# Last batch: routing steps, ranks and row sends reordered against halves of the shared expert

## The reference, cut to what matters

```python
x = x + xattn(layernorm(x), ctx, ctx, ...)
f = layernorm(x)
logits = f @ Wg
gates = softmax over the two largest logits, 0 elsewhere
y = sum over e of (silu(f @ W1[e] + b1[e]) * (f @ W11[e] + b11[e]) @ W2[e] + b2[e]) * gates[:, e]
z = silu(f @ Ws1 + bs1) * (f @ Ws11 + bs11) @ Ws2 + bs2
x = x + y + z
```

## Time and profile before

| what | value |
|---|---|
| median of 3 runs | 305.14 us (305.01 to 306.45) |
| the profiled execution | 304.97 us, its span 303.2 us |
| PE busy | 272.4 us (90% of the span) |
| DVE busy | 206.7 us (68%) |
| ACT busy | 150.2 us (50%) |
| POOL busy | 141.9 us (47%) |

### The profile page before, as it was taken

How to read it: one execution, slowest core, us unless ns; L and a number is a source line. 1 busy time by engine, 2 the same in 40 slices (tenths; PEclk the granted TensorE clock), 3 DMA queues, 4 the chain that set the end, 5 groups by cost and what they waited for, 6 DMA issues and landing times.

```text
span 303.2 us, 6139 instructions
## 1 busy us (share of the span) xinstructions
PE 272.4 (90%) x1829; PEld 204.7 (68%) x1845; DVE 206.7 (68%) x724; ACT 150.2 (50%) x316; POOL 141.9 (47%) x228
## 2 busy tenths in 40 slices
PE   7777899999998999989998999999789999999910
PEld 7554555666565665565564467898689999999900
DVE  3869455665857678775796468773267787878863
ACT  3434787655664574746554754322145454544500
POOL 3484614654233307843347303755026566666740
PEclk9999999999999999999999999999999999999975
DMA  6999940929890000100001100118625959777446
GB/s 207 378 366 395 406 190 1 108 33 136 308 383 11 2 1 0 38 18 20 0 2 36 36 1 8 51 42 269 196 55 151 288 186 286 254 237 229 105 191 208
DMA packets 28495, 44.22 MB, mean 146 GB/s; under 512 B 2752, under 2 KB 16192, under 8 KB 28464
## 3 DMA queue, kind: packets, MB, share of 16 engines
q1 hardware_dynamic: 21808, 36.52, 36.0%
q0 software_dynamic: 6656, 7.31, 10.9%
HBM read 27.00 MB, written 14.73 MB: 138 GB/s over the span
## 4 chain that ended last, share of the span: by engine, by line
PE 64%; DVE 14%; DMA 8%; POOL 5%; issue 5%; ACT 3%; POOLq 0%; DVEq 0%; ACTq 0%; SPq 0%
PE ps L1470 6%; PE ps L1476 6%; PE ps L1487 6%; DVE mpad L587 6%; PE ps L1190 5%; PE ps L1218 5%; PE ps L1232 5%; PE ps L1191 4%; PE ps L1228 4%; POOL slot_rows L866 3%; PE ps L1216 3%; PE ps L1203 3%; DMA result_rows<-yo,dest 3%; PE ps L1139 2%; PE ps L1141 2%
## 5 line engine op out<-in xcount | busy, mean ns | idle before, releaser
L587 DVE TENSOR_REDUCE mpad<-ps 128x2 f32<-128x312 f32 x128 | 55.8, 477 | 35.5 <-PE ps L1191 35.2
L937 POOL DMA_INDIRECT result_rows<-yo,dest x47 | 45.3, 964 | 39.0 <-DVE yo L790 38.1
L816 POOL TENSOR_SCALAR ks<-k_stack,cst 128x160 fp32r<-128x160 f32 x64 | 30.0, 483 | 70.9 <-DVE k_stack L560 70.9
L1002 ACT ACTIVATE pf<-ps 128x512 f32<-128x512 f32 x80 | 46.6, 597 | 15.0 <-PE ps L1232 10.8
L1191 PE MATMUL ps<-ks,qs 96*128 96x312 f32 x128 | 47.2, 411 | 0.0
L1190 PE MATMUL ps<-mq_b,identb 128*128 128x312 bf16 x128 | 38.1, 303 | 5.6 <-POOL ks L816 3.2
L866 POOL DMA_INDIRECT slot_rows<-xr,slot x32 | 31.5, 984 | 14.2 <-issue 13.9
L1218 PE MATMUL ps<-qs,ks 128*128 128x512 f32 x64 | 37.1, 582 | 0.0
L1190 PEld LDWEIGHTS ps<-mq_b,identb 128*128 128x128 bf16 x128 | 12.3, 96 | 34.9 <-issue 30.5
L1126 ACT ACTIVATE e_s<-ps,wu 128x128 f32<-128x128 f32 x62 | 19.4, 364 | 21.8 <-PE ps L1470 21.8
L1487 PE MATMUL ps<-wd,e_h 128*128 (+1 forms) x188 | 28.7, 276 | 0.6 <-DVE yo L790 0.6
(11 more groups left out here) (194 smaller groups left out, 602.6 us busy)
## 6 DMA issues: line engine op xcount, KB each, us to landing
wu<-w_biased SPq DMA_DIRECT2D x31, 322.0 KB, 3.9
wr<-w_up SPq DMA_DIRECT2D x1, 5152.0 KB, 24.7
w_biased<-wr SPq DMA_DIRECT2D x1, 5152.0 KB, 16.9
slot_rows<-zero SPq DMA_DIRECT2D x1, 3120.0 KB, 26.9
xg<-slot_rows SPq DMA_DIRECT2D x12, 260.0 KB, 3.9
wd<-w_down SPq DMA_DIRECT2D x1, 2048.0 KB, 12.0
xo<-result_rows SPq DMA_DIRECT2D x3, 512.0 KB, 5.3
xs<-bor POOLq DMA_DIRECT2D x1, 1024.0 KB, 11.3
```

The lines of the kernel that those rows point to most:

```text
L587: dve.tensor_reduce(mpad[:, m % 2, q, 96 + 2 * a:98 + 2 * a], ps[:, KS_ + a, 0:2 * SKM].rearrange("p (c k) -> p c k", c=2), AX.X, ALU.max, ...
L816: pool.tensor_scalar(ks[:, HG * (m % 4) + j, :], k_stack[:, m % 2, :], cst[:, C_SELM + j:C_SELM + j + 1], cst[:, C_SELO + j:C_SELO + j + 1 ...
L937: pool.indirect_dma_start(out=result_dram[:, :], out_offset=bass.IndirectOffsetOnAxis(ap=dest[:, n:n + 1], axis=0), in_=yo[:, n % 4, :], i ...
L1002: act.activation(pf[:, n % RP, :], ps[:, ST_ + n % 2, :], ACT.Exp, scale=DK ** -0.5).then_inc(exp_done, 1)
```

## The change

Nothing is computed differently, and no instruction is added. Orders change on four engines: on DVE the slots of batch 2 go ahead, the statistics and the normalization of batch 3 go ahead of products, and the slots of batch 3 are put around product 6, ahead of product 7; on POOL three sends of batch 2 go ahead of the inverse deviation; on ACT one small activation is moved; on PE the turn, the logits and the ranks go ahead of halves, the second layer of batch 2 is split by three halves, and the wait for the last add moves behind the third up-projection.

```diff
--- before.py
+++ after.py
@@ -721,31 +721,32 @@
 
             last = B - 1
             gates(last - 1)
-            slots(last - 1, 0)
+            for step in range(3):
+                slots(last - 1, step)
             normalize(last, NG - 1)
-            slots(last - 1, 1)
+            slots(last - 1, 3)
             linear_half(0)
-            slots(last - 1, 2)
-            slots(last - 1, 3)
+            slots(last - 1, 4)
             add_attention(last, 0)
+            batch_statistics(last, 0)
             linear_half(1)
-            batch_statistics(last, 0)
             linear_half(2)
+            next_blocks(last - 1)
+            batch_norm(last, 0)
             linear_half(3)
-            batch_norm(last, 0)
-            slots(last - 1, 4)
+            batch_low(last, 0)
             linear_half(4)
-            batch_low(last, 0)
-            next_blocks(last - 1)
-            linear_half(5)
             read_logits(last)
             for step in range(4):
                 pick(last, step)
+            linear_half(5)
+            gates(last)
+            for step in range(3):
+                slots(last, step)
             linear_half(6)
-            gates(last)
+            for step in range(3, 5):
+                slots(last, step)
             linear_half(7)
-            for step in range(5):
-                slots(last, step)
             linear_half(8)
             tile_experts()
             linear_half(9)
@@ -927,8 +928,9 @@
             split_weights(1)
             for b in range(B):
                 batch(b)
+            send(B - 2, range(3))
             batch_inverse_std(B - 1, 0)
-            send(B - 2, range(2 * QT))
+            send(B - 2, range(3, 2 * QT))
             send(B - 1, range(2 * QT))
 
 
@@ -1103,8 +1105,8 @@
             batch_high(B - 1, 0)
             silu(5)
             copy_rows(B - 1, 0)
+            gate_exp(B - 1)
             silu(6)
-            gate_exp(B - 1)
             silu(7)
             for k in range(8, 16):
                 silu(k)
@@ -1418,14 +1420,14 @@
             first(2)
             first(3)
             first(4)
+            turn_normed(B - 1, 0)
             first(5)
-            turn_normed(B - 1, 0)
+            logits(B - 1, 0)
             second(0, (0, 1))
-            logits(B - 1, 0)
+            first(6)
+            rank_rows(B - 1)
             second(0, (2, 3))
-            first(6)
             first(7)
-            rank_rows(B - 1)
             first(8)
             first(9)
             second(1, (0, 1))
@@ -1435,9 +1437,9 @@
             first(11)
             first(12)
             second(2, (0, 1))
-            second(2, (2, 3))
             for k in range(13, 16):
                 first(k)
+            second(2, (2, 3))
             second(3, (0, 1))
 
 
@@ -1492,7 +1494,6 @@
             pe.wait_ge(x2_done, B - 1)
             turn_rows(0)
             second(3, (2, 3))
-            pe.wait_ge(x2_done, B)
             pe.wait_ge(tile_known, 1)
             pe.wait_ge(ld_d, 32)
             experts = {0: expert_of(0)}
@@ -1503,6 +1504,8 @@
                     up(n)
                 if 1 <= n < RUN:
                     experts[n] = expert_of(n)
+                if n == 2:
+                    pe.wait_ge(x2_done, B)
                 if n >= 2:
                     down(n - 2, experts.pop(n - 2))
 
```

## The result

The changed kernel takes **308.01 us** (median of 17 runs, 306.36 to 310.47) against 305.37 us for the kernel before in its 17 runs: a ratio of 1.0091, 95% interval 1.0066 to 1.0117. It is slower by more than the half per cent that can be told. The forecast was 306.7 with a range up to 307.9: the direction of the sum was right, the size was missed just beyond the edge.

The account below looks back on a forecast made before the run. Bound: the chain of sends, row load, turn and experts. A later tile list delays the row load; with the moved wait, experts at 222.1 instead of 220.57, +1.55; 304.75 becomes 306.5, median 0.17 above: 306.7, range 305.3 to 307.9.

Parts of the forecast that it names:

- The order of the passage: Attention to experts: times of the reordered steps, from batch 2's slots at 180.3 to the tile list published at 206.5.
- other signs of being right: Rows issued right behind the eighth weight load, near 216, long after the last send; no wait between last piece and experts.
- The rows' landing: First row load behind the weight loads: lands 3.9 us after its issue at 215.9, so the turn is at 219.9.
- The last piece: Second-layer piece on PE between the turn and the experts: 1.75 us, within the 2.2 from turn to experts.
- What moves 220.57 moves the end by as much: Start of the experts, 220.57 before: PE's expert matmuls follow without a gap, so a shift there moves the end equally.
- Stops added up: PE ahead of the tile list: new stops 1.3 + 0.8 + 0.3 + 1.1, less 0.2, put the one-row matmul 3.25 us later.
- The gain of these sends is nil: POOL's three early sends of batch 2: without them all of batch 2's sends would be over before 195 anyway.
- The moved wait: Wait for the last add, behind the third up-projection: turn to experts 2.2 instead of 3.20 us, one microsecond won.
- Floor landing: Rival: the row load lands 2.9 us after issue, 305.7 us in all; chance 0.20.
- the list in time: Rival "faster": PE's stops don't reach the tile list, published by 203.3; sends decide again, 303.2 us; chance 0.07.
- The port rule: Rival "slower still": DVE's normalization and POOL's send shut each other out, row load to tile list 0.97 later, 307.7; chance 0.15.
- that rival's condition: Sign for the slower rival, 307.7 us: it decides as soon as a send starts ahead of the normalization; chance 0.15.

Follow-up runs that it names:

- the second profile: The changed kernel, nothing altered, timed and profiled once more: 307.53 us against 305.19 for the kernel before, ratio 1.0095; the profiled execution took 306.27 us.
- the first profile: The changed kernel's profile from its first timing: execution of 307.83 us, span 306.0 us, against 304.97 and 303.2 us for the kernel before.

## Why the prediction missed

**The order of the passage: right.** The forecast is named first, the measured time behind it. Slots of batch 2 at 180.3 (180.05), inverse deviation behind three sends done at 186.0 (185.7), half 3 at 183.5 (183.12), turn at 187.2 (187.07), logits at 189.4 (189.22), ranks at 193.6 (193.34), slots at 198.7 (198.44), half 9 at 199.5 (199.24), one-row matmul at 205.95 (205.70), list at 206.5 (206.05 and 0.20). With the earlier start of 0.39 added back, each is within 0.3 us. The stops ahead of halves 3 and 9 were 1.42 and 0.84 us for 1.3 and 1.1. Its other signs of being right came true too: the row load behind the eighth weight load, the sends long landed, no wait between the last piece and the experts.

**The rows' landing: mis-sized, and this is the step that failed first.** The prediction took 3.9 us, the middle of twelve issues, on the ground that three sends fewer run beside it. Measured: 4.87, and 4.61 in the second profile. The twelve issues were the wrong sample, as they reach down to 272 us, far into the experts, and most don't stand behind eight weight loads: in the changed kernel the engines are 0.92 busy over 216 to 218.4 and 0.71 in the 2 us after, and with that the rows land. An earlier issue did not help either (5.90 with the sends put back, though the engines were 0.41 busy over 218 to 220 us there, for 0.87 in the changed kernel), so the backlog alone does not give the number. The bound of 5.7 in the prediction held all but that one; the value inside it was chosen too low.

**The last piece: priced at the wrong clock.** "Experts at 219.9 + 2.2" takes the piece at 1.75 us from a row at full clock. The prediction had PE waiting from 218.6 to 219.9, 1.3 us, and it named a fallen clock as what would break the durations, but gave it neither a price nor a chance. This is the term that took the time out of its range: the second profile has the long landing with the clock held, and its execution took 306.27 us. With the longer landing the wait was 2.03 us; the piece took 3.23 us (221.12 to 224.35) and the turn ahead of it 0.65 for 0.46. From the forecast's experts at 222.1: 0.44 earlier for the issue, 0.97 later for the landing, 0.19 for the turn and 1.48 for the piece make 224.3, against 224.35 measured. In the second profile, with the clock held, 0.22 less and 0.71 more make 222.6, against 222.68.

**"What moves 220.57 moves the end by as much": nearly.** The experts begin 2.11 us later in the second profile and 3.78 in the first, and the spans grow by 1.3 and 2.8. What is given back is in DVE's waits near the end, 0.77 us of it in the first profile and 0.41 in the second in the wait for scattered results shown above. The prediction read the chain's rows up to PE's last matmul and not the wait behind it. This hid the landing's error in the executions that kept the clock: their median, 306.87, and the second profile's span, 304.5 for 304.75 forecast, come out close to the sum, partly by two errors that cancel.

**Stops added up: right in sum, wrong in cause.** The 1.3 of half 3 was put down to the statistics ahead of product 1. With that undone nothing came back, because POOL's early sends hold up the normalized rows anyway. "The gain of these sends is nil" was right but half of it: they cost the tile list 1.1 us.

**The moved wait, one microsecond: right**, by the kernel that has it alone.

**The rivals.** Floor landing and the list in time did not happen. The port rule gave 307.7 by another mechanism, and its number came nearer than the forecast for no good reason: the normalization took 1.20 us beside a send that starts at 185.91, behind it, and 1.12 with none before. In the run with the sends put back a send starts at 184.00, ahead of the normalization at 184.04, which was that rival's condition, and the normalization took 1.13 us. The Trainium skill, "SBUF — State Buffer", "Who interferes with whom", has DVE in a two-port mode and GpSimd shut each other out for a whole instruction; these rows leave room for 0.1 us. Whether these instructions ran in such a mode no row says.

## What to carry to other kernels

When a change makes TensorE wait longer, price the work behind the wait at both granted clocks, and give the lower one a chance: here the wait's second price, 1.5 us, was as much as the forecast had as its whole loss. A load that is queued behind others is priced from issues that stand behind the same loads, and not from the median of all its issues: 4.1 us was the one such row before, 4.6 to 5.9 the range after. And whatever starts the longest transfers, here a one-row matmul, goes ahead of work that nobody is waiting for: moving it ahead of one piece and one half was worth as much as the whole change had lost. And before a profile is compared with another, look for stretches of lower granted clock in both, at every place: here one such stretch in the attention moved whole profiles by 1.1 to 1.5 us.

## What the hardware did that was not expected

At the turn of the first rows the granted clock fell after idle times of 2.03, 2.36 and 3.09 us, and the piece behind took 3.0 to 3.5 us; it held after 0.53, 0.73, 1.36, 1.59 and twice 1.88 (the changed kernel's second profile, and the one with product 1 moved). The changed kernel ran both ways, so its median is a mixture, and single profiles of it can differ by 1.5 us with nothing else changed. The idle time just before is not all that decides: near 28.4 us PE was idle for 0.72 us in the profile with 8 products of zeros and in that of the kernel before, and the clock fell in the first and held in the second. What decided there these rows do not show. The Trainium skill, "TensorE: Matmul & The Clock Gate", Part 1, describes a gate whose default is the lower clock and which activity opens; the windows agree in the order of things, 0.50 only after PE had stood idle, with PE busy through it from 221 us on, and 0.93 again over 224 to 225.

The row load's landing, 4.6 to 5.9 us when it was issued right behind the eighth weight load, did not follow its issue: issued at 214.36 it landed at 220.26, issued at 215.46 at 220.33. Why the earlier one took 1.0 us longer, with its weight loads earlier by as much and the engines emptier over 218 to 220 us, is not settled by these runs.
